# Norm phase between FFN and gated delta attention: statistics and scaling on two engines, two row tiles kept in SBUF, first weights prepared inside the norm

## The reference

```python
x = x + 0.5 * ffn(layernorm(x))      # weights 2048x512, 2048x512, 512x2048, from cubic splines
x = x + attn(layernorm(x))
x = x + 0.5 * ffn(layernorm(x))      # the same ffn weights
# attn: qkvz = x @ W_qkvz; b, a = x @ W_ba; causal conv of 4 taps and silu on q, k, v
# beta = sigmoid(b); g = -exp(A_log) * softplus(a + dt_bias)
# per head (16 key heads, 32 value heads, 128 wide) over 512 steps:
#   S = S*exp(g); delta = (v - k@S)*beta; S += outer(k, delta); o = q@S
# out = (silu(z) * rms_norm(o) * norm_w) @ W_out
```

## Time and profile before

| | |
|---|---|
| median of 3 runs | 3748.13 us (3747.31 to 3750.79) |
| the profiled execution's own time | 3746.4 us |
| its span, first to last instruction | 3744.6 us |
| granted TensorE clock, mean | 0.976 of full speed |
| TensorE matmul busy | 3522.7 us, 94% |
| VectorE, ScalarE, GpSimd busy | 56%, 56%, 60% |

### The profile page before, as it was taken

One profiled execution on the slowest core, in us unless ns is written; L12 is line 12 of the kernel. 1 busy time (PEld: TensorE's weight loads), 2 busy tenths in 40 slices (PEclk: granted clock), 3 DMA queues, 4 the chain that ended last, 5 costly groups with the idle time before them and its releaser, 6 DMA issues. The chain is left out here.

```text
span 3744.6 us, 76942 instructions
## 1 busy us (share of the span) xinstructions
PE 3522.7 (94%) x29092; PEld 2941.4 (79%) x29092; DVE 2110.6 (56%) x4091; ACT 2081.8 (56%) x5616; POOL 2233.1 (60%) x2645
## 2 busy tenths in 40 slices
PE   5996599999999999999999999999999999996898
PEld 3884388888888888888888888888888888885787
DVE  4654355555555555555555555555555555552564
ACT  3442266666666666666666666666666666663343
POOL 2101467676767676767676767677777777762110
PEclk8998799999999999999999999999999999997999
DMA  4314112121212121212121212121212121210421
GB/s 152 116 35 83 61 53 74 64 74 64 74 64 74 64 74 64 74 64 75 68 76 64 75 66 80 67 75 64 78 66 80 63 75 67 71 57 35 163 57 35
DMA packets 207871, 270.34 MB, mean 72 GB/s; under 512 B 86160, under 2 KB 117264, under 8 KB 206352
## 3 DMA queue, kind: packets, MB, share of 16 engines
q1 hardware_dynamic: 202464, 250.02, 20.4%
q0 software_dynamic: 4464, 14.36, 1.0%
q10 hardware_dynamic: 576, 1.03, 0.1%
HBM read 176.05 MB, written 89.13 MB: 71 GB/s over the span
## 5 line engine op out<-in xcount | busy, mean ns | idle before, releaser
L1892 ACT ACTIVATE at_t<-at_inv 128x512 f16<-128x512 f32 x768 | 460.2, 599 | 509.2 <-PE at_inv L1701 509.2
L1480 PE MATMUL at_proj<-x_hi,at_w_hi 128*128 128x512 f32 x1024 | 437.6, 427 | 18.0 <-POOL at_w_lo L2151 18.0
L1480 PE MATMUL at_proj<-x_hi,at_w_lo 128*128 128x512 f32 x1024 | 421.5, 412 | 0.0
L1480 PE MATMUL at_proj<-x_lo,at_w_hi 128*128 128x512 f32 x1024 | 415.6, 406 | 0.0
L2230 POOL TENSOR_TENSOR at_gt_lo<-at_cst,at_gates 128x512 fp32r<-128x512 f32 x256 | 261.9, 1044 | 250.2 <-PE at_misc L1480 250.2
L2077 DVE TENSOR_TENSOR at_pml<-at_prod,at_cst 128x256 f16<-128x256 f32 x768 | 322.8, 420 | 147.4 <-PE at_prod L1480 136.5
L2047 DVE TENSOR_TENSOR at_rows<-at_misc,at_rows 128x512 f32<-128x512 f32 x256 | 177.0, 692 | 282.3 <-PE at_misc L1480 281.7
L1480 PE MATMUL at_prod<-at_t,at_nlhi 128*128 128x64 f16 (+1 forms) x3584 | 287.3, 197 | 24.7 <-ACT at_t L1890 13.3
L1480 PE MATMUL at_proj<-at_w_hi,x_hi 128*128 128x256 f32 x1024 | 308.5, 301 | 0.8 <-DVE at_cv_q L2002 0.8
L1480 PE MATMUL at_proj<-at_w_hi,x_lo 128*128 128x256 f32 x1024 | 308.0, 301 | 0.0
L1480 PE MATMUL at_proj<-at_w_lo,x_hi 128*128 128x256 f32 x1024 | 302.3, 295 | 0.0
(11 more groups left out here) (290 smaller groups left out, 10631.3 us busy)
## 6 DMA issues: line engine op xcount, KB each, us to landing
at_rows<-x SPq DMA_DIRECT2D x64, 1024.0 KB, 5.6
x<-at_rows SPq DMA_DIRECT2D x64, 1024.0 KB, 4.2
at_gb<-decays SPq DMA_DIRECT2D x64, 512.0 KB, 3.7
at_raw<-w_qkvz SPq DMA_DIRECT2D x46, 512.0 KB, 3.6
ffn_weights<-ffn_w SPq DMA_DIRECT2D x1, 11776.0 KB, 36.8
ffn_w<-ffn_weights POOLq DMA_DIRECT2D x4, 2688.0 KB, 23.3
at_raw<-w_out SPq DMA_DIRECT2D x16, 512.0 KB, 3.5
f_xnext<-x_in SPq DMA_DIRECT2D x4, 1024.0 KB, 5.2
```

What stands on the lines that cost most here:

```text
L1480: return nc.tensor.matmul(out, lhsT, rhs, start=start, stop=stop)
L1892: own["a_t"].up(A(grown(t16[:, s % R].rearrange("p a t -> p (a t)"), s // R), grown(psT[s % R], s // R), ACT.Copy))
```

## The change

1. Both FFNs' and the splines' clearing blocks are spread over five engines. The norm's semaphores, not cleared before, are cleared behind the attention, by SP (20) and VectorE (19).
2. First FFN: SP loads x1 tiles 0 and 1 into `rows` while later tiles are computed. The last tile's 16 stores go half from SP, half from ScalarE's queue, and the block ends without waiting for them.
3. Norm: rows 0 to 7 are read from `rows`; the fourth quarter of x1 is loaded once the stores are in. VectorE keeps `bn_stats`, `bn_aggr` and `low`; GpSimd adds eps, raises to the power and makes `shift`; ScalarE scales. `turn` has three banks. `gates_of` takes the products with x_hi first. The tail works in two halves of the tokens, with the running sum before the tail sum, and both before g's split.
4. Norm: SP also loads the attention's constants, taps and first weights, and GpSimd splits the weights behind its chunks. The block ends without waiting for `gates` and `decays`; SP waits for each in the attention, ahead of its first load of it.
5. Attention: units 0 and 1 use `rows` as they are, without a load.

```diff
 def ffn_phase(...)
                     if w_known:
-                        for a, b, n in runs:
+                        for a, b, n in runs[0::2] if t == NT - 1 else runs:
                             sp.dma_start(yv[t][:, :, a:a + n], xres[:, :, b:b + n]).then_inc(y_out, 16)
...
                     load_res(t)
+                    if 1 <= t <= len(rows):
+                        sp.dma_start(rows[t - 1][:], yv[t - 1]).then_inc(rows_in[t - 1], 16)
...
                 store(NT - 1)
-                sp.wait_ge(y_out, STORED * NT)
...
+                if w_known:
+                    act.wait_ge(y_done, 4 * NT)
+                    for a, b, n in runs[1::2]:
+                        act.dma_start(last[:, :, a:a + n], xres[:, :, b:b + n]).then_inc(y_out, 16)
 def norm_phase(...)
             @block.sync
+                sp.dma_start(cst[:], cst_in[:, 0:C_LATER]).then_inc(ident_in, 16)
+                sp.dma_start(later[:], cst_in[:, C_LATER:C_END]).then_inc(consts_in, 16)
                 sp.wait_ge(half_set, 2)
...
+                sp.dma_start(resid[:, 0:CH, :], xv[2]).then_inc(x_in[2], 16)
+                sp.dma_start(cst16[:], cst16_in).then_inc(more_in, 16)
+                sp.dma_start(nw[:], norm_w.rearrange("(p a) -> p a", a=1)).then_inc(more_in, 16)
+                sp.wait_ge(stored, all_stored)
+                sp.dma_start(resid[:, CH:2 * CH, :], xv[3]).then_inc(x_in[3], 16)
+                for i in range(3):
+                    sp.dma_start(raws[i][:], w_qkvz[...]).then_inc(raw_in[i], 16)
+                load_taps(sp, conv_w, cw_raw, 0, taps_in)
...
-                sp.wait_ge(gates_out, 16)
-                sp.wait_ge(decay_out, 16)
+                sp.wait_ge(more_in, 32)
             @block.gpsimd
                 for c in range(NCH):
                     pool.wait_ge(stats_done, c + 1)
-                    nc.gpsimd.tensor_tensor(rstd[:, c:c + 1], mv[:, c, 1:2], half[:, c:c + 1], ALU.pow).then_inc(rstd_done, 1)
+                    nc.gpsimd.tensor_scalar(mv[:, c, 1:2], mv[:, c, 1:2], EPS_LN, None, ALU.add).then_inc(plink, 1)
+                    pool.wait_ge(plink, 2 * c + 1)
+                    nc.gpsimd.tensor_tensor(rstd[:, c:c + 1], mv[:, c, 1:2], half[:, c:c + 1], ALU.pow).then_inc(plink, 1)
+                    pool.wait_ge(plink, 2 * c + 2)
+                    nc.gpsimd.tensor_scalar(shift[:, c:c + 1], mv[:, c, 0:1], rstd[:, c:c + 1], -1.0, ALU.mult, ALU.mult).then_inc(rstd_done, 1)
+                    if c == 3:
+                        pool.wait_ge(consts_in, 64)
...
             @block.scalar
+                def scale(c):
+                    act.wait_ge(rstd_done, c + 1)
+                    if c >= 3:
+                        act.wait_ge(turned, c - 2)
+                    nc.scalar.activation(normed[:, c % 3, :], chunk(c), ACT.Identity, bias=shift[:, c:c + 1],
+                                         scale=rstd[:, c:c + 1]).then_inc(normed_done, 1)
...
+                for c in range(NCH):
+                    scale(c)
+                    if c == 2:
+                        act.wait_ge(consts_in, 64)
+                        nc.scalar.activation(nega[:], nega[:], ACT.Exp).then_inc(exp_a, 1)
+                    if c >= 1:
+                        high(c - 1)
             @block.tensor
                 def gates_of(b, late=lambda: None):
-                    pe.wait_ge(xlo_done, (b + 1) * CH)
+                    pe.wait_ge(xhi_done, (b + 1) * CH)
                     for j in range(HB):
                         nc.tensor.matmul(out, ba_hi[:, j, :], x_hi[:, j, at], start=(j == 0), stop=False)
+                        nc.tensor.matmul(out, ba_lo[:, j, :], x_hi[:, j, at], start=False, stop=False)
+                    late()
+                    pe.wait_ge(xlo_done, (b + 1) * CH)
+                    for j in range(HB):
+                        last = nc.tensor.matmul(out, ba_hi[:, j, :], x_lo[:, j, at], start=False, stop=(j == HB - 1))
...
-                pe.wait_ge(g_done, 1)
+                pe.wait_ge(mul_done, 1)
 def attn_phase(...)
+            sp.wait_ge(gates_out, 16)
             load_gates(0)
-            load_part(sp, 0, 0, "l_kq", raw_e)
-            load_part(sp, 0, 1, "l_v", raw_g)
-            load_part(sp, 0, 2, "l_z", raw_w)
-            sp.wait_ge(sems["p_w"], 2)
+            sp.wait_ge(decay_out, 16)
             load_decays(0)
-            load_rows(0)
...
-                if not has_delta:
-                    for part in range(2):
-                        split_part(0, part)
...
                     mask_g(0)
-                    if not has_delta:
-                        split_part(0, 2)
```

328 lines of the change are left out of this document (182 added, 146 removed).

## The result

The changed kernel took 3704.66 us (median of four runs, 3703.08 to 3708.96) where the kernel before, run beside it, took 3748.10: a ratio of 0.9886 with a 95% interval of 0.9873 to 0.9898. Measured again beside the first experiments it took 3706.97 against 3746.53, ratio 0.9893 (0.9878 to 0.9907). The forecast was 3701.5 with a range of 3693 to 3712.

A forecast was written before the change was run, and what follows sets the result against it. TensorE, busy 94% of the span, was the bound, so time could come only from its idle stretches. Savings of 44.6 us on the path plus 2.0 elsewhere, 46.6, gave 3701.5 us; range 3693 to 3712.

The forecast's parts named there:

- the first rival: Norm: the 16 chunks keep their old pace and take 39.0 us; time 3712.5 us, chance 0.17.
- five pieces: Path from last FFN1 result to attention's first product: to first transpose, chunks, gates to product, to last store's issue, to attention.
- Piece 1: Last FFN1 stores to the norm's first transpose: 25.6 us before, transpose at 348.4 instead of 361.4, 13.0 us saved.
- The upper bound, 352: Norm's first transpose comes as late as 352 us if two store queues take 3.5 us more than one.
- Piece 2: Norm's chunks, first transpose to last x_hi: 39.0 us before, 27.6 at VectorE's period of 1.55, 11.4 us saved.
- the start's brake: Norm's start: GpSimd's weight split and ScalarE's exponential wait for constants; chunk 4 scaled from 352.9, first transpose at 348.4.
- Piece 3: Gates' tail, last x_hi to last store's issue: 19.9 us before, 16.1 by working in halves, 3.8 us saved.
- Piece 4: Last store's issue to attention's first product: 16.9 us before, one block change of 0.5 left, 16.4 us saved.
- The second rival: Norm's tail: GpSimd's splits collide with VectorE's operations, tail up to 8 us longer; 3709.5 us, chance 0.06.
- the slower case: Attention: new SBUF places and DMA phase make each unit longer; at 1.0 us a unit 3765 us, chance 0.03.
- that rival's transpose at 353: Norm's start: the block's end waits for the stores after all, first transpose at 353; 3706 us, chance 0.05.
- The rest: Outside the path: attention's second mask 1.1 us sooner, semaphore clears 1.5 saved and 0.6 lost; 2.0 us saved.

The follow-up runs named there:

- one_queue: Changed kernel with all 16 stores of the first FFN's last tile issued by SP again, still not awaited; 3707.71 us, ratio 0.9895 to before.
- rows_loaded: Changed kernel with the first two blocks' rows loaded from memory in the norm, ahead of the constants, not in FFN1; 3710.60 us, ratio 0.9901 to before.
- two_tiles: Changed kernel with two transpose tiles and two scaled rows in the norm instead of three, x_lo earlier again; 3714.89 us, ratio 0.9915 to before.
- scale_on_vector: Changed kernel with the eps addition and the scaling back on VectorE, GpSimd computing the power alone; 3709.42 us, ratio 0.9897 to before.
- third_late: Changed kernel with GpSimd's split of the first weights' third part held until `gates_done` reaches 2; 3708.23 us, ratio 0.9897 to before.
- weights_in_attention: Changed kernel with the first weights loaded and split in the attention again, as before the change; 3715.12 us, ratio 0.9911 to before.

## Why the prediction was right, and where it was off

The path was right, and three of its four savings were put too high: 44.6 us forecast, 36.8 measured. The time itself came out only 3.2 us above the forecast, and that is in part luck: the saving of 43.4 us in the first measurement was 39.6 in the second, and against the 46.6 that were forecast it is the second that shows what the path lacks. The range reached to 3712 for the sake of the first rival, which did not come. Point by point:

- **The bound.** The path was the right one: five pieces, 101.5 us, and 36.8 of the 40 to 43 us that the time fell by lie in it. The rest, some 3.7 us between the means of the spans, lies nearly all in the attention and FFN2; see the last point.
- **Piece 1, 13.0 us forecast, 10.2 and 10.5 measured.** The term that failed is "I take about the old landing": the stores were complete 15.2 us behind their start and not 12.7, and the identity with them, at 15.4. The upper bound, 352, was the value. Its reason, that two queues take longer than one, held in small part: in one_queue, with SP alone, the stores were complete at 14.7 us, only 0.5 to 1.4 sooner. Why they take longer than the 12.7 and 13.9 us of before when nobody awaits them stays open. Two terms beside it were too small: an issue beside the other queue's was 0.80 us and not 0.56, and the norm began 8.1 us behind the stores' start, not 5.9. Neither mattered, for the wait on the identity covered both. Of what the piece did gain, 5 us are the kept rows (rows_loaded); the other 5 should be the stores' landing that FFN1's end no longer awaits, which no run tested by itself.
- **Piece 2, 11.4 forecast, 8.4 measured.** The period was not the weak term (1.43 for 1.55). The weak one was that three chunks cover one burst "nearly", with 3.5 us added for three bursts: ScalarE waited 7.0 and 6.6 us for transposes behind the gate products, in three waits. About 1 us more is the start's brake: chunk 4 was scaled 5.6 us behind the first transpose, where 4.5 were forecast. (ScalarE's two operations a chunk took 0.81 and 0.58 us, not 2 x 0.6, and so it stood as full as VectorE.) The prediction named the third tile and the bursts and still summed by VectorE's period; two_tiles and scale_on_vector show that without the tile nothing is gained, and that the lighter VectorE gives 1.9 of the 8.4 us, only together with it. The first rival, chunks at the old pace, did not come, but two_tiles shows how near it was.
- **Piece 3, 3.8 forecast, 1.5 measured** (1.3 and 1.8). Up to the product 10.3 were forecast and, without the splits, 10.2 measured: the working was right, and the collision added 1.2 to 1.7. From there to the end 5.8 were forecast and 6.7 measured, where the last issue took 1.90 us for 0.36.
- **Piece 4, 16.4 forecast, 16.4 measured.** By the runs 10.7 of it are the weights and 4.3 the stores not awaited; if the two add up, 1.4 are left for the other loads that moved.
- **The second rival, chance 0.06, happened**, at 1.2 to 1.7 us and not at 8. Its price was overstated because two or three operations met a split and most of their wait fell into idle time. But it was dismissed by rows that could not speak of it. The prediction held that 64 operations with two SBUF inputs had kept their length. In the attention of the kernel before, every operation of VectorE that ran beside one of the 63 splits reads a PSUM tensor, as this one does:

```profile
601.50 2.37 POOL L2151 TENSOR_TENSOR at_w_lo<-at_raw,at_w_hi 128x1024 fp32r<-128x1024 f32 x1
...
602.94 0.75 DVE L2002 SCALAR_TENSOR_TENSOR at_cv_k<-at_proj,at_cw,at_cv_k 128x511 f32<-128x511 f32 x1 [0.72 <-ACT at_cv_k L1817]
```

  The 64 operations of L2011 never met one. So these rows could not tell whether VectorE is held. The Trainium skill, SBUF — State Buffer (Who interferes with whom), says that an operation of VectorE with at most one SBUF input, outside its two-port modes, does not contend with GpSimd; this agrees with x_lo at 384.55 to 385.24 of third_late, which kept its 0.69 us beside a split's cast, and with the reciprocals' 1.75 us, the same beside a split (388.31 in the second profile of the change) and without one (weights_in_attention).
- **The other rivals.** The units kept their length, so nothing of the slower case came. The norm's start did not wait for the stores; that rival's transpose at 353 came true within a microsecond, by another cause, the identity's landing.
- **The rest, 2.0 us forecast.** FFN1 paid nothing for the two loads, as forecast. The attention's first 42 us (to VectorE's sixth write of `at_cv_q`) took 40.3 us in both profiles for 42.1 and 42.3: 1.8 to 2.0 us gained for 1.1. From the last matmul to FFN2's first load it took 8.6 us for 7.8: 0.8 lost for 0.6. Behind the splines it took 1.4 us for 1.8: 0.4 gained, near the forecast's 0.5. Behind FFN2's last matmul it took 6.9 us to the end for 8.4: 1.5 gained for 1.0. That is some 3.0 us of these terms for 2.0. The rest of the 3.7 is no term of the prediction: 1.2 us of it are the clock, since both profiles of before have the slower of the two patterns told below and the change has one of each, and FFN2 took some 0.9 us more up to its last matmul.
- **The signs.** Two of the prediction's own signs of being wrong are to be read here. The identity landed at 352.2 us, behind the 351 that it had set. And it would have looked for the collision in a split above 2.6 us: no split of the change was that long (2.43 at most), while VectorE's operations were; the sign watched the wrong engine. The landmarks came 3 to 9 us later than said (first statistics at 345.0 for 342, last x_hi at 382.7 for 376, first product at 401.8 for 392.6), 1.1 us of which is FFN1's later end in that profile.
